# Depthwise products of images 2 to 4 from half-precision high and low parts

## The chip, the core and the metric

The kernel runs on one core of one Trainium2 chip. The metric is the device time of one execution in microseconds (us), the median of several runs. A core has five engines that run their own instruction streams and meet at semaphores: TensorE (PE, with its weight loads listed as PEld), VectorE (DVE), ScalarE (ACT), GpSimd (POOL) and SyncE (SP, which here only issues DMAs).

## The reference

Input x holds 4 images of 96 channels and 128 x 128 pixels, in 32-bit floats. Two residual layers follow one another. The change touches the first.

```
x = x + L0(groupnorm(x))      # channel attention
x = x + L1(groupnorm(x))      # five convolutions, folded into one 5x5

L0:  xn = layernorm over the channels, with weight and bias
     q  = dwconv3x3(conv1x1(xn, q_w),  q_dw)      # 96 channels
     kv = dwconv3x3(conv1x1(xn, kv_w), kv_dw)     # 48 channels: k 24, v 24
     q, k = l2norm over the 16384 pixels of each channel
     attn = softmax(q k^T * temperature)          # 8 heads, 12 x 12 each
     out  = conv1x1(attn v, proj_w)
```

dwconv3x3 is a depthwise convolution: each of the 144 channels has its own 3 x 3 kernel and is padded with zeros. It is the operation that the change rewrites.

## The kernel before

The four images go through the same stages one after another. X, the current image, stays in on-chip memory (SBUF) as 96 channels x 16384 pixels.

**Projection.** For each of 32 tiles of 4 image rows ACT normalises (L1025), PE multiplies by the folded weights (L796), ACT squares and takes roots, DVE scales by the inverse deviation (`scaled`, L1402), and POOL adds the bias and writes the tile transposed into `Q` (`biased`, L640). In `Q` the 128 partitions are the pixel columns of the image, and the free axis is 144 channels x 128 rows. DVE writes the last tile itself (L1396).

**Depthwise stage.** The convolution along the partitions is a product with a 128 x 128 matrix with three diagonals (a band matrix). One channel takes three products, one for each vertical tap, summed in PSUM: `mm` at L817, L818 and L819, all in 32-bit floats, with the moving operand shifted by one row for the upper and the lower tap. Channels go in 24 chunks of 6 (`DC`, `DK`), two chunks to a turn of the loop. Per chunk:

- DVE makes 18 band matrices by one multiplication of the taps, spread out, with a mask (`bands`, L1428); two chunks of matrices have room (`T`), so the next `bands` of a buffer waits until PE is done with the chunk two before (`s_dw`).
- PE makes 18 products into one of two pairs of PSUM banks, and waits for the matrices (`s_T`), and for the eviction and the low part of the chunk two before (`s_qd`, `s_qkl`).
- ACT stores the result (`evict`, L1065): for q and k (chunks 0 to 19) as a 16-bit high part in `HL`, for v (chunks 20 to 23) as 32-bit floats into `Q` (L1062).
- For q and k DVE stores what the rounding left as a 16-bit low part (`low_parts`, L1437). DVE's order in the loop is `bands` of chunk n, then `low_parts` of chunk n-2.

Between its evictions ACT sums the next image's rows for its statistics (L1074, L1082), which SP loads at the same time. In image 1 POOL cuts the convolution weights into parts during this stage (`split_weights`, L596 to L615); in images 2 to 4 POOL does nothing in it.

**Attention.** DVE gathers strips (L1453), PE makes q k^T from the 16-bit parts (`gram`, L845), ACT copies v into strips (`values`, L1104) that PE turns (L837), DVE and ACT make the softmax (L1482 to L1505, L1128), PE applies it (L879) and DVE adds it to X (L1514).

**Convolution.** 11 units of rows per image; PE works from 16-bit parts (L957), with DVE, ACT, POOL and DMAs making and placing the parts.

Before image 1 a setup turns the depthwise taps into the layout of the matrices (POOL L572 to L578), with a scale from `QKS` that DVE works out (L1306 to L1315). POOL starts `biased` of image 1 after its last step.

The order on each engine is written out by hand, with a semaphore for each hand-over; there is no planner.

Of the kernel before, what the change touches and what calls it, by code (L numbers as in the profile page):

```python
# [25 lines left out]
def build_program(nc, x, ln_w, ln_b, q_w, q_dw, kv_w, kv_dw, proj_w, temperature, w1, w3, w5, wd, wf, out):  # L26
    f32, f16, bf16, i32 = mybir.dt.float32, mybir.dt.float16, mybir.dt.bfloat16, mybir.dt.int32
    ALU = mybir.AluOpType
# [22 lines left out]
    BW = 129  # L51
    GR = 8
# [8 lines left out]
    WTOP = 1024.0  # L61

# [33 lines left out]
    with ctx:  # L96
# [12 lines left out]
        def plain_sem(name):  # L109
# [11 lines left out]
        Q_AT = SLOT  # L121
        WORK_AT = Q_AT + WORK
        Q = region[:, Q_AT:WORK_AT].rearrange("p (c h) -> p c h", c=CO)
# [11 lines left out]
        V = sb("V", [P, 3, 3 * CO])  # L135
        band = sb("band", [P, BW])
# [4 lines left out]
        small = sb("small", [P, 48])  # L141
# [7 lines left out]
        pq = region[:, 0:2 * AR * CO].rearrange("p (i r c) -> p i r c", i=2, r=AR)  # L149
        y1 = work[0:C, 0:AD * BANK].rearrange("p (i n) -> p i n", i=AD)  # L150
        sq = [t.rearrange("p (r c) -> p r c", r=AR) for t in (region[:, 1152:1152 + AR * C], work[:, 2048:2048 + AR * C])]
        vr, sd, rr = (work[:, a:a + AD * AR].rearrange("p (i r) -> p i r", i=AD) for a in (2432, 2448, 2464))
# [3 lines left out]

        T = work[:, 1536:1536 + 2 * DM * BW].rearrange("p (i m x) -> p i m x", i=2, m=DM)
        vT = work[:, 0:AT * P]
# [7 lines left out]
        KEPT = VPAIRS - EARLY  # L166
        vs = [t.rearrange("p (r c) -> p r c", r=VR) for t in
              [region[:, GROUPS_QK * SLOT + k * VR * VP:GROUPS_QK * SLOT + (k + 1) * VR * VP] for k in range(3)] +
# [3 lines left out]
        assert len(vs) == KEPT and GROUPS_QK * SLOT + 3 * VR * VP <= Q_AT + QK * H  # L172
        VBANK = (1, 2, 1, 2, 4, 5, 6, 7)

        Qf = region[:, Q_AT:WORK_AT]

# [61 lines left out]
        tapsum = Qf[:, 10200:10200 + QK]  # L238
# [7 lines left out]
        QKS, CLAMP, WMAX, TMAX, BMAX = 43, 44, 45, 46, 47  # L246
        MEANX, VARX, SAX, SBIX, MG2 = 23, 24, 27, 28, 29
# [35 lines left out]
        s_T = sem("band_matrices")  # L283
        s_dw = sem("depthwise_chunk")
# [49 lines left out]
        N_BOUND, N_RES, N_QKS, N_AMAX, N_WSC = 6, 9, 17, 22, 25  # L334
# [3 lines left out]
        NPOOL = 18  # L338
# [181 lines left out]
        def _(pool):  # L520
            n = [0]

            def link(ins):
# [18 lines left out]
            link(pool.memset(band[:], 1.0))  # L542
            link(pool.affine_select(out=band[:], in_=band[:], compare_op=ALU.is_ge, fill=0.0, base=1,
                                    pattern=[[-1, BW]], channel_multiplier=1))
# [20 lines left out]
            for j in range(3):  # L565
                if j == 2:
                    pool.wait_ge(s_st, N_AFF + START)
                for d in range(3):
# [5 lines left out]
                    if d:  # L574
                        turning.done(pool.tensor_tensor(V[:, j, :], V[:, j, :], turned, ALU.add))
                        pool.wait_ge(s_V, turning.value())
# [1236 lines left out]
```

## Time and profile before

| | |
|---|---|
| time of 3 runs, us | 1709.13 (1708.07 to 1710.19) |
| span of the profiled execution, us | 1706.1 (its own run time is not recorded beside it) |
| busy share of the span | PE 97%, PEld 91%, DVE 87%, ACT 60%, POOL 34% |
| mean granted TensorE clock | 0.975 of full speed |
| HBM traffic | 52.20 MB read, 25.17 MB written |

The span runs from the first to the last instruction. A busy share is the time in which at least one instruction of the engine was open; matmuls are pipelined, so a busy PE need not be at its peak. A group names the source line, the engine and the operation, then output and input, and after the bar the busy time and the mean of one instruction in ns, then the idle time before it and what ended it. The lines of the pieces are shares of the chain of work that ended last.

### The profile page before, as it was taken

How to read it: one execution, taken by the hardware profiler on the slowest of the kernel's cores; microseconds unless marked ns; L12 is line 12 of the kernel's file. 1: busy time of each engine (PE TensorE's matmuls, PEld its weight loads, DVE VectorE, ACT ScalarE, POOL GpSimd, SP SyncE). 2: the span in 40 equal slices, each digit the busy share in tenths (PEclk: the TensorE clock that was granted, in tenths of full speed). 3: DMA queues.
4: the chain of work that ended last, by engine and by line, in shares of the span. 5: the costliest groups of instructions: out<-in, count | busy, mean ns of one | idle time of the engine just before them, and what ended most of it. 6: DMA issues, size and time to landing. Idle time of an engine off the chain costs nothing.

```text
span 1706.1 us, 38231 instructions
## 1 busy us (share of the span) xinstructions
PE 1652.5 (97%) x13285; PEld 1552.1 (91%) x13285; DVE 1488.7 (87%) x1964; ACT 1022.2 (60%) x1665; POOL 579.8 (34%) x398
## 2 busy tenths in 40 slices
PE   6999999999999999999999999999999999999998
PEld 6989959999999996999999996899999999599998
DVE  6788879999888859999978886999988887799997
ACT  4856576555385658545546666755446566765551
POOL 4999931222281003232247002123326400312222
PEclk9999979999999997999999999899999999799999
DMA  7012115666502201666630220366661121055553
GB/s 192 0 47 65 38 32 136 177 164 172 153 2 61 69 19 44 157 167 172 169 95 15 69 65 1 87 165 175 167 165 46 35 73 41 1 133 139 135 144 104
DMA packets 105017, 166.01 MB, mean 97 GB/s; under 512 B 40266, under 2 KB 78763, under 8 KB 104780
## 3 DMA queue, kind: packets, MB, share of 16 engines
q1 hardware_dynamic: 81772, 138.95, 32.0%
q10 hardware_dynamic: 23168, 26.04, 4.7%
q8 instruction: 47, 0.77, 0.2%
q14 instruction: 30, 0.25, 0.0%
HBM read 52.20 MB, written 25.17 MB: 45 GB/s over the span
## 4 chain that ended last, share of the span: by engine, by line
PE 84%; DVE 7%; issue 4%; ACT 3%; DMA 1%; DVEq 0%; SPq 0%; POOL 0%; ACTq 0%; POOLq 0%
PE ps L957 41%; PE ps L796 12%; PE ps L817 8%; PE ps L819 7%; PE ps L818 7%; PE ps L845 3%; PE ps L879 3%; PE ps L952 1%; PE ps L752 1%; ACT region L1178 1%; DVE region L1706 1%; DVE region L1676 1%; ACT region L1111 1%; DVE X L1514 1%; DVE region L1673 1%
## 5 line engine op out<-in xcount | busy, mean ns | idle before, releaser
L957 PE MATMUL ps<-region,W 128*96 128x256 f16 (+2 forms) x7140 | 800.7, 270 | 10.0 <-DMA region<-region 5.4
L957 PEld LDWEIGHTS ps<-region,W 128*96 128x96 f16 (+1 forms) x7140 | 771.3, 122 | 31.8 <-issue 14.8
L1428 DVE TENSOR_TENSOR region<-V,band 128x2322 f32<-128x2322 f32 (+2 forms) x104 | 257.8, 2488 | 59.5 <-PE ps L819 56.1
L1178 ACT ACTIVATE region<-region 96x1584 f16<-96x1584 f32 (+2 forms) x80 | 98.4, 1272 | 309.1 <-DVE region L1610 309.1
L701 POOL TENSOR_TENSOR region<-region 96x528 f32<-96x528 f32 (+1 forms) x72 | 92.0, 1282 | 445.9 <-DVE region L1676 328.4
L817 PE MATMUL ps<-region 128*128 (+1 forms) x1152 | 228.1, 280 | 10.4 <-DVE region L1428 4.5
L819 PE MATMUL ps<-region 128*128 (+1 forms) x1152 | 222.8, 275 | 0.0
L818 PE MATMUL ps<-region 128*128 (+1 forms) x1152 | 222.2, 274 | 0.0
L1706 DVE SCALAR_TENSOR_TENSOR region<-ps,small,region 96x768 f32<-96x768 f32 (+1 forms) x220 | 203.7, 988 | 12.1 <-PE ps L957 10.4
L796 PE MATMUL ps<-proj,region 96*128 96x240 f32 x1024 | 209.3, 367 | 0.6 <-DVE region L1402 0.6
L796 PEld LDWEIGHTS ps<-proj,region 96*128 96x128 f32 x1024 | 194.8, 191 | 14.1 <-DVE region L1402 1.0
L640 POOL TENSOR_TENSOR region<-region,cbias 128x576 f32 (+1 forms) x124 | 175.6, 1419 | 56.7 <-DVE region L1402 53.3
L817 PEld LDWEIGHTS ps<-region 128*128 128x128 f32 x1152 | 174.6, 191 | 16.9 <-issue 15.2
L691 POOL TENSOR_TENSOR region<-region,X 96x1536 f32<-96x1536 f32 x40 | 116.1, 2903 | 197.0 <-DVE region L1737 197.0
L1676 DVE TENSOR_TENSOR region<-region 96x1056 f16<-96x1056 f32 (+6 forms) x160 | 175.4, 1154 | 0.0
L819 PEld LDWEIGHTS ps<-region 128*128 128x128 f32 x1152 | 174.8, 192 | 0.0
L818 PEld LDWEIGHTS ps<-region 128*128 128x128 f32 x1152 | 174.8, 192 | 0.0
L667 POOL TENSOR_TENSOR region<-X 96x512 f32<-96x512 f32 (+1 forms) x16 | 29.2, 1844 | 385.1 <-PE ps L879 385.1
L1065 ACT ACTIVATE region<-ps 128x768 f32 (+1 forms) x80 | 65.8, 823 | 137.2 <-PE ps L819 137.2
L1172 ACT ACTIVATE region<-region 96x1584 f16<-96x1584 f16 (+3 forms) x88 | 114.0, 1296 | 0.3
L1402 DVE TENSOR_TENSOR region<-ps,region 128x576 f32<-128x576 f32 x124 | 94.0, 758 | 15.0 <-DVE region L1392 1.9
L1025 ACT ACTIVATE region<-X,small 96x512 f32 (+1 forms) x128 | 101.6, 802 | 0.3 <-DVE small L1330 0.3
(234 smaller groups left out, 2199.8 us busy)
## 6 DMA issues: line engine op xcount, KB each, us to landing
region<-region SPq DMA_DIRECT2D x104, 247.5 KB, 3.9
region<-in_x_dram SPq DMA_DIRECT2D x128, 192.0 KB, 2.3
out_dram<-region SPq DMA_DIRECT2D x40, 576.0 KB, 4.2
region<-region ACTq DMA_DIRECT2D x72, 247.5 KB, 2.4
X<-in_x_dram SPq DMA_DIRECT2D x30, 576.0 KB, 6.2
region<-region SPq DMA_DIRECT2D x32, 247.4 KB, 4.9
X<-in_x_dram SPq DMA_DIRECT2D x19, 384.0 KB, 10.6
region<-region SPq DMA_DIRECT2D x24, 185.6 KB, 3.7
```

The source lines that it names most:

```text
L640: pool.tensor_tensor(Q[:, :, bass.ds(t * AR, AR)].rearrange("p c r -> p r c"), pq[:, i], cbias[:].unsqueeze(1).broadcast_to([P, AR, CO]), ...
L691: pool.tensor_tensor(ob[:, 0:r * W], ob[:, 0:r * W], X[:, bass.ds(u * UR * W, r * W)], ALU.add).then_inc(s_res, 1)
L796: last = mm(ps[:, 2 * i + r // 2, r % 2 * 256:r % 2 * 256 + NP], y1[:, i, r * W:(r + 1) * W], proj[:], start=True, stop=True)
L817: mm(o, T[:, i, 3 * c + 1, 0:W], src, start=True, stop=False)
L818: mm(o[:, 1:H], T[:, i, 3 * c, 0:W], src[:, 0:H - 1], start=False, stop=False)
L819: last = mm(o[:, 0:H - 1], T[:, i, 3 * c + 2, 0:W], src[:, 1:H], start=False, stop=True)
L957: last = mm(o, w, src, start=k == 0, stop=k == len(steps) - 1, skip_group_check=split and ck > 0)
L1172: act.activation(hi2[0:C, a:e, x:z], hi[0:C, a:e, x:z], ACT.Copy).then_inc(s_h, 1)
L1178: act.activation(dst[0:C, a:e, x:z], src, ACT.Copy, scale=1.0 if whole else col(SA)).then_inc(s_h, 1)
L1428: v.tensor_tensor(T[:, i, 3 * c:3 * c + m].rearrange("p m (i j) -> p m i j", j=3), taps.broadcast_to([P, m, BW // 3, 3]), mask.broadcast_t ...
L1676: v.tensor_tensor(low[:, :, x:end], src, hi[0:C, a:e, x:end], ALU.subtract).then_inc(s_l, 1)
L1706: step = lambda dst, g, factor, src: v.scalar_tensor_tensor(row(dst), product(i, g, blocks), col(factor), row(src), ALU.mult, ALU.add).the ...
```

## The change

The depthwise products of images 2 to 4 (`b` > 0) run on 16-bit operands. A value is cut into a high and a low 16-bit part, and a product of 32-bit values becomes three products: high matrix x high values, high matrix x low values, low matrix x high values. Image 1 keeps the 32-bit products.

- PE: 54 products of 16-bit operands per chunk in place of 18 of 32-bit operands.
- POOL (`query_split`): per chunk a copy of 768 values per partition into 16 bits (`QH`, two buffers), then the subtraction of it from the 32-bit values, written as 16 bits (`QL`, in the place of the chunk in `Q`). It waits until PE is done with the chunk two before. Chunk 0 goes in three parts.
- DVE (`bands`): per chunk two multiplications of 16-bit operands with 16-bit results of 18 x 132 elements per partition, in place of one with 32-bit operands of 18 x 129. The mask `band` is kept in 16 bits; taps are stored with the three horizontal taps next to each other (`V`).
- `low_parts` becomes one scalar_tensor_tensor (scale, then subtract), `evict` takes a scale; six channels lie next to each other in two PSUM banks.
- At the end of image 1's depthwise stage DVE cuts the taps into parts once (three instructions).
- Setup: DVE scales the projection weights and bias (two instructions) and keeps gains for taps and values apart; POOL's last step scales all taps (1296 elements, before 1080) and writes them in the new order.
- Buffers: `Q` begins 768 elements earlier, and between it and `work` lies room for `QH`. `pq`, `y1`, `sq` and the small statistics move. The strips of v have five buffers (before six); `values(7)` comes after the load of ACT's exponential table.

```diff
+        QH = span(EXTRA_AT, DC * H).bitcast(f16).rearrange("p (i c h) -> p i c h", i=2, c=DC)
+        QL = span(Q_AT, WORK).bitcast(f16).rearrange("p (n e) -> p n e", n=DK)[:, :, 0:DC * H].rearrange("p n (c h) -> p n c h", c=DC)
+        T16 = work[:, 1536:1536 + 2 * DM * BW16].bitcast(f16).rearrange("p (i k m x) -> p i k m x", i=2, k=2, m=DM)
...
-            turning.done(pool.tensor_scalar(V[:, :, 0:3 * QK], V[:, :, 0:3 * QK], col(QKS, P), None, ALU.mult))
+            turning.done(pool.tensor_scalar(Vf[:], Vf[:], col(TAPGAIN, P), None, ALU.mult))
...
+                def query_split(k2, i, parts):
+                    n = k2 * 2 + i
+                    done = (b - 1) * DK + n
+                    pool.wait_ge(s_dw, b * DK + n - 1 + START)
+                    for at, (c, channels) in enumerate(parts):
+                        rows = Q[:, bass.ds(n * DC + c, channels), :]
+                        high = QH[:, i, c:c + channels]
+                        step = len(PARTS_OF_T) // len(parts)
+                        pool.tensor_copy(high, rows).then_inc(s_qh, step)
+                        pool.wait_ge(s_qh, done * len(PARTS_OF_T) + (at + 1) * step + START)
+                        pool.tensor_tensor(QL[:, bass.ds(n, 1), c:c + channels].rearrange("p o c h -> p (o c) h"), rows, high,
+                                           ALU.subtract).then_inc(s_qsp, step)
+                if b > 0:
+                    pool.wait_ge(s_q, (b + 1) * (AT - 1) + START)
+                    pool.wait_ge(s_pq, (b + 1) * AT + START)
+                    query_split(0, 0, PARTS_OF_T)
+                    query_split(0, 1, ((0, DC),))
+                    with pool.Fori(1, DK // 2) as k2:
+                        for i in range(2):
+                            query_split(k2, i, ((0, DC),))
...
                                 pe.wait_ge(s_T, n * len(PARTS_OF_T) + ready + START)
+                                if b:
+                                    pe.wait_ge(s_qsp, (n - DK) * len(PARTS_OF_T) + ready + START)
...
+                            if b:
+                                high = QH[:, i, c]
+                                low = QL[:, bass.ds(k2 * 2 + i, 1), c].rearrange("p o h -> p (o h)")
+                                for tap, to, x in ((1, 0, 0), (0, 1, 0), (2, 0, 1)):
+                                    n_ = H - to - x
+                                    for part, src in ((0, high), (0, low), (1, high)):
+                                        last = mm(o[:, to:to + n_], T16[:, i, part, 3 * c + tap, 0:W], src[:, x:x + n_],
+                                                  start=(tap, part) == (1, 0) and src is high, stop=(tap, part) == (2, 1))
+                                continue
...
-                for k in range(KEPT, VPAIRS):
+                for k in range(KEPT, VPAIRS - 1):
                     values(k)
...
                 act.activation(col(TMAX), epsc[0:C, 0:1], ACT.Exp)
+                values(VPAIRS - 1)
                 act.wait_ge(s_st, sv + N_NMX + START)
...
+            link(setup, v.tensor_scalar(col(TAPGAIN, P), col(TAPGAIN, P), TAPTOP, None, ALU.mult))
+            link(setup, v.tensor_scalar(col(QGAIN, P), col(QGAIN, P), QTOP, None, ALU.mult))
+            link(setup, v.tensor_scalar(proj[:, 0:CO], proj[:, 0:CO], col(QGAIN), None, ALU.mult))
+            link(setup, v.tensor_scalar(cbias[:], cbias[:], col(QGAIN, P), None, ALU.mult))
...
+                        if b:
+                            wide = mask16.rearrange("p (i j) -> p i j", j=3).unsqueeze(1).broadcast_to([P, m, BW16 // 3, 3])
+                            for part in range(2):
+                                taps = V16[:, bass.ds(k2 * 2 + i, 1), 1 - part, 9 * c:9 * c + 3 * m] \
+                                    .rearrange("p o (m j) -> p (o m) j", j=3).unsqueeze(2)
+                                step = v.tensor_tensor(T16[:, i, part, 3 * c:3 * c + m].rearrange("p m (i j) -> p m i j", j=3),
+                                                       taps.broadcast_to([P, m, BW16 // 3, 3]), wide, ALU.mult)
+                            step.then_inc(s_T, len(PARTS_OF_T) // len(parts))
+                            continue
...
-                    v.tensor_tensor(part(GC), ps[:, 4 + 2 * i:6 + 2 * i, 0:3 * H].rearrange("p k (c h) -> p h k c", c=3), part(0),
-                                    ALU.subtract).then_inc(s_qkl, 1)
+                    v.scalar_tensor_tensor(part(GC), chunk_of(i).rearrange("p (c h) -> p h c", c=DC),
+                                           HLSCALE, part(0), ALU.mult, ALU.subtract).then_inc(s_qkl, 1)
...
+                if b < 1:
+                    whole_taps = Vf[:].rearrange("p (n e) -> p n e", n=DK)
+                    dve.wait_ge(s_T, DK * len(PARTS_OF_T) + START)
+                    v.tensor_copy(VH, whole_taps).then_inc(s_vsp, 1)
+                    dve.wait_ge(s_vsp, 1)
+                    v.tensor_tensor(V16[:, :, 0], whole_taps, VH, ALU.subtract).then_inc(s_vsp, 1)
+                    dve.wait_ge(s_vsp, 2)
+                    v.tensor_copy(V16[:, :, 1], VH).then_inc(s_vsp, 1)
```

## Rows read from the trace of the kernel before

**Rows 1.** The page: the span, and the chain that ended last by line.

```profile
span 1706.1 us, 38231 instructions
...
PE ps L957 41%; PE ps L796 12%; PE ps L817 8%; PE ps L819 7%; PE ps L818 7%; PE ps L845 3%; PE ps L879 3%; PE ps L952 1%; PE ps L752 1%; ACT region L1178 1%; DVE region L1706 1%; DVE region L1676 1%; ACT region L1111 1%; DVE X L1514 1%; DVE region L1673 1%
```

**Rows 2.** Windows, image 2's depthwise stage: length, PE, PEld, DVE, ACT, POOL, clock, DMA.

```profile
519.00:618.40 99.40, 98.42 (x866) 97.40 (x865) 80.86 (x53) 61.17 (x152) 0.04 (x1) 1.00 0.22 64
```

**Rows 3.** Timeline, both ends of that stage: start, us, engine, line.

```profile
517.65 1.34 DVE L1396 SCALAR_TENSOR_TENSOR region<-ps,region,cbias 128x144 f32<-128x144 f32 x4
...
519.19 5.20 DVE L1428 TENSOR_TENSOR region<-V,band 128x387 f32<-128x387 f32 x4 [0.20 <-DVE region L1396]
...
618.59 6.75 PE L845 MATMUL ps<-region 128*120 128x240 f16 x64
```

**Rows 4.** The chain in order of time: start, us, stretches of 16-bit products.

```profile
300.95 18.52 PE ps L957 x163
...
618.73 6.61 PE ps L845 x64
...
1688.61 6.98 PE ps L957 x83
```

**Rows 5.** Groups by shape in image 2's depthwise stage, DVE alone.

```profile
L1428 DVE TENSOR_TENSOR region<-V,band 128x2322 f32<-128x2322 f32 x23 | 59.3, 2578 | 14.8 <-PE ps L819 14.3 <-issue 0.5
...
L1437 DVE TENSOR_TENSOR region<-ps,region 128x768 f32 x20 | 19.0, 952 | 0.0
...
L1453 DVE COPY region<-region 128x1920 f16<-128x1920 f16 x4 | 2.5, 640 | 3.7 <-PE ps L819 3.7
```

**Rows 6.** Timeline of POOL in image 1's depthwise stage.

```profile
103.01 2.80 POOL L611 TENSOR_TENSOR W<-W 96x192 f32<-96x192 f32 x1
105.89 2.81 POOL L612 TENSOR_TENSOR W<-W 96x192 f32<-96x192 f32 x1
108.77 0.82 POOL L613 CAST W<-W 96x768 f16<-96x768 f32 x1
...
137.28 1.64 POOL L615 TENSOR_TENSOR W<-W 96x768 f16<-96x768 f32 x1
...
165.25 3.85 POOL L615 TENSOR_TENSOR W<-W 96x768 f16<-96x768 f32 x1
```

**Rows 7.** Timeline of the setup, POOL and DVE.

```profile
24.55 1.25 DVE L1306 TENSOR_REDUCE region<-region 128x120 f32<-128x1080 f32 x1
...
41.07 1.59 POOL L572 TENSOR_SCALAR V<-region,small 128x432 f32<-128x432 f32 x1 [5.06 <-DVE small L1330]
...
44.42 1.10 POOL L575 TENSOR_TENSOR V<-V,region 128x432 f32<-128x432 f32 x1
...
48.50 3.02 POOL L578 TENSOR_SCALAR V<-V,small 128x1080 f32<-128x1080 f32 x1
...
53.01 0.76 DVE L1402 TENSOR_TENSOR region<-ps,region 128x576 f32<-128x576 f32 x1 [1.78 <-POOL region L640]
```

**Rows 8.** Timeline of DVE in image 1's depthwise stage.

```profile
99.87 8.38 DVE L1428 TENSOR_TENSOR region<-V,band 128x387 f32<-128x387 f32 x5 [0.20 <-DVE region L1396]
108.17 0.94 DVE L1437 TENSOR_TENSOR region<-ps,region 128x768 f32 x1
...
137.84 3.52 DVE L1428 TENSOR_TENSOR region<-V,band 128x2322 f32<-128x2322 f32 x1 [1.11 <-PE ps L819]
...
164.53 3.07 DVE L1428 TENSOR_TENSOR region<-V,band 128x2322 f32<-128x2322 f32 x1 [1.33 <-PE ps L819]
```

**Rows 9.** Timeline of ACT in image 2's attention.

```profile
619.52 4.73 ACT L1104 ACTIVATE region<-region 128x384 f32<-128x384 f32 x6
...
635.75 0.20 ACT L1126 ACTIVATE small<-epsc 96x1 f32<-96x1 f32 x1
...
636.18 0.31 ACT L1128 ACTIVATE region<-region,small 96x24 f32<-96x24 f32 x1 [0.23 <-DVE small L1498]
```

**Rows 10.** Windows of image 1's depthwise stage and image 2's attention, for the clock.

```profile
640.00:656.00 16.00, 15.43 (x57) 4.44 (x50) 16.00 (x29) 13.85 (x16) 13.76 (x13) 0.65 0.01 2
...
120.00:140.00 20.00, 18.23 (x161) 17.86 (x161) 17.41 (x9) 12.79 (x34) 19.18 (x12) 1.00 0.20 59
```

More of the change, by code:

```diff
@@ L134, in build_program @@
         proj = sb("proj", [C, NP])
-        V = sb("V", [P, 3, 3 * CO])
-        band = sb("band", [P, BW])
+        Vf = sb("V", [P, 9 * CO])
+        V = Vf[:].rearrange("p (m j) -> p m j", j=3)
+        V16 = Vf[:].bitcast(f16).rearrange("p (n k e) -> p n k e", n=DK, k=2)
+        band = sb("band", [P, BW16], f16)
         ident = sb("ident", [P, P])
@@ L140, in build_program @@
         cbias = sb("cbias", [P, CO])
-        small = sb("small", [P, 48])
+        small = sb("small", [P, 52])
         nsums = sb("nsums", [C, 2 * AT])
@@ L146, in build_program @@
         ps = ctx.enter_context(nc.psum_tensor("ps", [P, 8, BANK], f32))
[L149 to L152, printed above, removed]
+        span = lambda at, n: region[:, at:at + n]
+        chunk_of = lambda i: ps[:, 4 + 2 * i:6 + 2 * i, :].rearrange("p k n -> p (k n)")[:, 0:DC * H]
+        pq = [span(at, AR * CO).rearrange("p (r c) -> p r c", r=AR) for at in (0, EXTRA_AT)]
+        SQ_AT = EXTRA_AT + AR * CO
+        Y1_AT = SQ_AT + AR * C
+        sq = [span(at, AR * C).rearrange("p (r c) -> p r c", r=AR) for at in (SQ_AT, Y1_AT + AD * BANK)]
+        y1 = region[0:C, Y1_AT:Y1_AT + AD * BANK].rearrange("p (i n) -> p i n", i=AD)
+        vr, sd, rr = (span(at, AD * AR).rearrange("p (i r) -> p i r", i=AD) for at in (576, 592, 608))
+        assert AR * CO <= 576 and 624 <= Q_AT
         stage = [work[0:C, j * BANK:(j + 1) * BANK] for j in range(3)]
@@ L165, in build_program @@
         EARLY = 2
-        KEPT = VPAIRS - EARLY
+        KEPT = 5
         vs = [t.rearrange("p (r c) -> p r c", r=VR) for t in
-              [region[:, GROUPS_QK * SLOT + k * VR * VP:GROUPS_QK * SLOT + (k + 1) * VR * VP] for k in range(3)] +
+              [span(GROUPS_QK * SLOT, VR * VP), span(EXTRA_AT, VR * VP)] +
               [work[:, AT * P + k * VR * VP:AT * P + (k + 1) * VR * VP] for k in range(3)]]
@@ L171, in build_program @@
         strip_at = lambda k: S[0] if k == 0 else S[1 + (k - 1) % 3]
-        assert len(vs) == KEPT and GROUPS_QK * SLOT + 3 * VR * VP <= Q_AT + QK * H
+        assert len(vs) == KEPT and GROUPS_QK * SLOT + VR * VP <= Q_AT + QK * H
         VBANK = (1, 2, 1, 2, 4, 5, 6, 7)
-        Qf = region[:, Q_AT:WORK_AT]
+        Qf = region[:, Q_AT:EXTRA_AT]
         RING = SLOTS * BLK
@@ L540, in _ @@
                                     pattern=[[CG, GROUPS], [0, CG]], channel_multiplier=-1))
[L542 to L546 removed]
+            link(pool.memset(wideband, 1.0))
+            link(pool.affine_select(out=wideband, in_=wideband, compare_op=ALU.is_ge, fill=0.0, base=1,
+                                    pattern=[[-1, BW16]], channel_multiplier=1))
+            link(pool.affine_select(out=wideband, in_=wideband, compare_op=ALU.is_ge, fill=0.0, base=1,
+                                    pattern=[[1, BW16]], channel_multiplier=-1))
+            link(pool.tensor_copy(band[:], wideband))
             link(pool.memset(res, 0.0))
@@ L570, in _ @@
                     turn = small[:, at:at + 1]
-                    product = turned if d else V[:, j, :]
+                    product = turned if d else V[:, :, j]
                     turning.done(pool.tensor_scalar(product, rawdw[:, :, d], turn, None, ALU.mult))
@@ L574, in _ @@
                     if d:
-                        turning.done(pool.tensor_tensor(V[:, j, :], V[:, j, :], turned, ALU.add))
+                        turning.done(pool.tensor_tensor(V[:, :, j], V[:, :, j], turned, ALU.add))
                         pool.wait_ge(s_V, turning.value())
             pool.wait_ge(s_dv, N_QKS)
-            turning.done(pool.tensor_scalar(V[:, :, 0:3 * QK], V[:, :, 0:3 * QK], col(QKS, P), None, ALU.mult))
+            turning.done(pool.tensor_scalar(Vf[:], Vf[:], col(TAPGAIN, P), None, ALU.mult))
             assert turning.n == N_TURNED
@@ L1305, in _ @@
             dve.wait_ge(s_taps, 3)
[L1306 removed]
+            link(setup, v.tensor_reduce(tapsum, rawdw.rearrange("p (c m) d -> p c (m d)", m=3), AX.X, ALU.add,
                                         apply_absolute_value=True))
@@ L1415, in _ @@
                     scaled(AT - AD + i, i, i == AD - 1)
+                mask16 = band[:]
                 def bands(k2, i, parts):
```

69 lines of the change are left out of this document (40 added, 29 removed).

## The prediction

> **What bounds the kernel now.** I read the page first: the chain that ended last runs over PE for most of its length; the largest piece is the convolution (L957), then the projection (L796), then the three lines of the depthwise products, 22% together [rows 1]. The change touches only these last. Then I cut out one depthwise stage, image 2's, by windows: PE is busy 98.42 of 99.40 us, DVE 80.86, ACT 61.17, POOL 0.04, at clock 1.00 [rows 2]. So PE is the bound there, at 98.42 / 24 = 4.10 us a chunk, and DVE is 81% full. The stage lasts from the end of L1396 (517.65 + 1.34 = 518.99) to the first gram product at 618.59: 99.6 us [rows 3]. Images 3 and 4 look the same; three such stages are changed. The question is which engine needs longest for a chunk afterwards.
>
> **PE, per chunk.** 18 products of 32-bit operands go, 54 of 16-bit operands with 128 columns come. No row has 16-bit products with 128 columns, but three dense stretches stand close: 256 columns 18.52 / 163 = 114 ns, 240 columns 6.61 / 64 = 103 ns, 192 columns 6.98 / 83 = 84 ns [rows 4]. At 2.4 columns per ns that is 107 + 7, 100 + 3 and 80 + 4. For 128 columns: 53 + 4 to 7, 57 to 60; I take 58 (nearest is the row of 192). The upper bound is 111, if the loading of 128 weight columns (another 53) were not hidden. A chunk: 54 x 0.058 = 3.13 us, bounds 3.1 and 6.0. PE alone would gain 0.97 us a chunk.
>
> **DVE, per chunk.** One band instruction goes (2578 ns for 2322 elements), two of 16 bits with 18 x 132 = 2376 elements come. The band row and the low-part row (952 ns for 768) give 1626 / 1554 = 1.046 ns an element and 149 ns fixed [rows 5]. Four band instructions of 387 + 774 + 1161 + 2322 elements would be 5.45 us by this and took 5.20 [rows 3]: each starts 0.085 before the one ahead of it ends. What a two-operand instruction costs with all operands in 16 bits, no row shows. Bounds: the 32-bit rate, 0.149 + 2376 x 1.046 ns = 2.63 us, and the rate of the 16-bit copy, 640 / 1920 = 0.333 ns an element, 0.79 us [rows 5]. The copy shows that 16-bit operands can pass several elements in the time of one of 32 bits; I take half of the 32-bit streaming time, the same bytes per ns: 0.149 + 1.24 = 1.39 us. Two of them and the low part (unchanged): 2 x (1.39 - 0.085) + 0.87 = 3.48 us, if nothing else uses the memory.
>
> The Trainium skill (VectorE: DVE Perf Modes, The perf-mode tier table) gives tensor_tensor two elements a cycle for 16-bit operands; by its figures this instruction takes about 1.4 us, and the sum would be the same.
>
> **POOL, per chunk, and the turns with DVE.** POOL is idle in the stage now; a copy into 16 bits and a subtraction with 16-bit result come. Image 1 has the same two forms with 768 elements: 0.82 us and 1.64 us, where they run free [rows 6]. These rows have 96 partitions; a 128-partition subtraction of 432 elements took 1.10 us [rows 7], which for 768 gives 1.96 as the upper bound. Free, POOL needs 0.82 + 1.64 + two gaps of 0.08 = 2.62 us a chunk, less than PE. But image 1's stage also shows what happens beside band instructions. A band instruction that starts at 137.84, while the subtraction of 137.28 still runs (until 138.92), takes 3.52 us and ends at 141.36: 2.44 after POOL is done, 0.14 less than a whole band instruction [rows 6, 8]. The other way, the subtraction of 165.25 beside the band instruction that ends at 164.53 + 3.07 = 167.60 takes 3.85 us and ends at 169.10: 1.50 after it, 0.14 less than its own 1.64. So the two do not share the memory: one waits for the whole of the other and saves only 0.14 us of its start. They take strict turns: through the run of five band instructions from 99.87 to 108.25 POOL's small instructions of 103.01 and 105.89 end 2.9 us apart, one behind each of the last two, the last 0.45 after DVE [rows 6, 8]. The low part isn't in it: L1437 at 108.17 and the copy at 108.77 overlap, and both take their usual 0.94 and 0.82 [rows 6, 8].
>
> In images 2 to 4 DVE has two band instructions and POOL two instructions a chunk, both always with the next one ready. A turn of the cycle: band 1.39 - 0.14 = 1.25, copy 0.68, band 1.25, subtraction 1.50; the low part (0.95) runs beside the subtraction. Sum 4.68 us a chunk, against 4.10 now. PE (3.13) and ACT (61.17 / 24 = 2.55) fit below it, and PE is done with a chunk before the next but one asks for its buffer, so nothing else lengthens the cycle. The gain of PE is not used: PE waits about 1.5 us in each chunk for parts.
>
> **One stage.** From 518.99: 0.2 to the first band instruction; chunk 0 in parts, like a cycle with eight more short instructions, 5.05 (estimate); 23 x 4.68 = 107.6; then PE's last chunk 3.13 and the small product after it 0.2. Sum 116.2 against 99.6: +16.6. Three stages: +49.9.
>
> **Setup, once.** DVE's reduction grows from 1080 to 1296 elements (1.25 us, +0.23) [rows 7]; three more small instructions in its chain, about 0.85 by the fixed 0.15 and 1.046 ns an element. POOL's first step of the last column waits for that chain, its last step grows from 3.02 to 3.62, and writes in the new order stand three elements apart: L572, which reads so, takes 3.7 ns an element where L575 takes 2.55 [rows 7], so up to 0.5 for each of two additions; I take 0.8. Sum 2.5, bounds 1.7 and 3. It is on the path: DVE stands 1.78 us at 53.01 for the first bias addition, which POOL starts after that step [rows 7]. DVE's cutting of the taps at the end of image 1's stage (three instructions, 2.8 us) lies beside PE's last two chunks; I count 0.5, bounds 0 and 1.
>
> **Softmax, four times.** `values(7)` (4.73 / 6 = 0.79 us) now runs after the table load, which ends at 635.95; the exponential started at 636.18 [rows 9]. It ends at about 636.75: +0.6, so 2.4 for four images. The other moves (buffers, six channels in a row, the scale in the eviction, one fewer strip buffer) change no instruction's size and add no late wait; 0.
>
> **Sum.** 49.9 + 2.5 + 0.5 + 2.4 = +55.3. The span of 1706.1 becomes 1761.4; the median of the runs lies 3.0 above the span, so 1709.1 + 55.3 = 1764 us. Own range 1745 to 1795: with 1.96 for the subtraction +22, with 0.25 us a chunk saved in the hand-overs -17.
>
> **Rivals.**
> - *No turns (faster).* The 16-bit band instructions leave POOL alone, or are so short that the turns fit. Without turns the stage is DVE's: 3.2 start, 20 x 3.48 + 3 x 3.13 (chunks without a low part, PE's pace) + 3.13 + 0.2 = 85.5, or -14.1 a stage; -42.3 + 5.4 gives 1672 us. It decides where a cycle falls below (99.6 - 1.8 - 8.6) / 23 = 3.88 us, so a band instruction below 0.99 us. For it: the copy's rate would do that. Against: all turns in rows 6 and 8 are between forms that read two operands, as these are. The Trainium skill (SBUF — State Buffer, SBUF: two separate sides) says that VectorE instructions with two SBUF inputs and GpSimd exclude one another for whole instructions, and it names no type; by it this rival falls. Chance 13%.
> - *Full-length 16-bit band instructions.* 2.63 us each: cycle 2 x 2.49 + 2.18 = 7.16, stage 0.2 + 7.5 + 164.7 + 3.3 = 175.7, +76; 1709.1 + 228 + 5.4 = 1943 us. For it: taps are spread by a repeated read of three elements, which no 16-bit row has. The Trainium skill (Vector Engine (DVE) Microarchitecture Reference, 5.1) has such instructions at one element a cycle when one element is read again and again; here three neighbours are. Chance 9%.
> - *PE becomes the bound.* Either weights aren't hidden or PE's waits of 1.5 us a chunk let its clock fall to 1.2 GHz: 111 ns a product, 6.0 us a chunk, stage 146, +46; 1709.1 + 139 + 5.4 = 1853 us. For it: clock 0.65 in a stretch with 57 products in 16 us; against it: 1.00 with PE busy 18.2 of 20 [rows 10], and here 54 dense products in every 4.7 us. Chance 7%.
> - The forecast: 71%.
>
> The range takes in the forecast's own and the faster rival, 1670 to 1800, and leaves out the other two (16%) and a little of the forecast. Within 0.2% (3.4 us, about what a measurement tells from no change) lies only a narrow piece between rival and forecast: 3%. Faster 11%, slower 86%.
>
> **What would show it.** Right: in images 2 to 4 POOL's subtractions and DVE's band instructions lengthened by each other, band instructions of about 1.4 us in their shortest, 4.7 us from chunk to chunk, PE idle about a third of the stage for POOL, stages of 116 us. Products 57 to 60 ns apart; gram of image 1 where it was, plus some 3 us. Wrong: band instructions never below 2.6 us; POOL instructions at 0.82 and 1.64 beside running band instructions; stages below 100 us; clock under 1 in the stage; or the difference outside these three stages.

## The result: 1843.9 us, slower by 7.9%

The changed kernel takes 1843.86 us (median of 4 runs, 1840.80 to 1847.21) against 1708.99 us: a ratio of 1.0787, 95% interval 1.0772 to 1.0802. The forecast was 1764 us, range 1670 to 1800. The direction was right; the loss is +135 us, not +55, and lies outside the range.

The page of the changed kernel, its first lines (busy us, share of the span, instructions; PEclk is the granted clock in 40 slices). PE falls to 6 or 7 in slices 12 to 14, 22 to 24 and 32 to 34, the depthwise stages of images 2 to 4, and there DVE stands at 9:

```profile
span 1839.1 us, 41682 instructions
...
PE 1638.7 (89%) x14581; PEld 1523.6 (83%) x14581; DVE 1666.2 (91%) x2045; ACT 1022.7 (56%) x1665; POOL 932.6 (51%) x555
...
PE   6999999999976679999997668999999777899998
...
DVE  6788889999899969999889996999988999699997
...
PEclk9999979999999997999998999799999888889999
```

Windows over the three changed stages (length, PE, PEld, DVE, ACT, POOL, clock, DMA). The first answers to [rows 2]:

```profile
525.40:667.20 141.80, 89.62 (x1299) 84.32 (x1298) 139.89 (x79) 61.35 (x152) 112.58 (x52) 0.92 0.15 45
982.00:1124.00 142.00, 91.56 (x1292) 86.10 (x1293) 138.94 (x78) 61.36 (x152) 112.80 (x50) 0.89 0.15 45
1438.00:1575.00 137.00, 96.79 (x1296) 91.97 (x1297) 132.97 (x78) 61.26 (x152) 121.90 (x51) 0.84 0.16 46
```

DVE went from 81% busy to all but full, PE from 99% to 63%: the bound has changed hands. (These busy times contain the wait for the other engine's turn.) Both ends of image 2's stage, as in [rows 3]:

```profile
523.98 1.35 DVE L1458 SCALAR_TENSOR_TENSOR region<-ps,region,cbias 128x144 f32<-128x144 f32 x4
...
667.26 0.91 PE L899 MATMUL ps<-region 128*120 128x240 f16 x7
```

From 525.33 to 667.24: 141.9 us, against 99.6. Measured the same way, images 3 and 4 take 143.4 and 138.1, against 100.0 and 100.6. That is +123.3 of the span's +133.0. Of the rest, 5.1 lies ahead of image 1's stage, 0.2 in it, and 4.4 in all that follows the four stages.

Groups of DVE in image 2's stage, busy us and mean ns, as in [rows 5]:

```profile
L1496 DVE TENSOR_TENSOR region<-V,band 128x2376 f16<-128x2376 f16 x46 | 117.1, 2588 | 0.0
L1510 DVE SCALAR_TENSOR_TENSOR region<-ps,region 128x768 f32 x20 | 18.7, 935 | 0.0
```

A mean of 2588 ns, nearly a whole 32-bit band instruction; but it mixes lengths. The timeline of image 2 shows single ones, DVE first, then POOL (start, us):

```profile
560.42 1.79 DVE L1496 TENSOR_TENSOR region<-V,band 128x2376 f16<-128x2376 f16 x1
562.14 3.21 DVE L1496 TENSOR_TENSOR region<-V,band 128x2376 f16<-128x2376 f16 x1
565.27 0.94 DVE L1510 SCALAR_TENSOR_TENSOR region<-ps,region 128x768 f32 x1
...
560.49 3.19 POOL L684 TENSOR_TENSOR region<-region 128x768 f16 x1 [0.20 <-POOL region L682]
565.68 0.82 POOL L682 CAST region<-region 128x768 f16 x1 [1.99 <-PE ps L867]
566.70 2.94 POOL L684 TENSOR_TENSOR region<-region 128x768 f16 x1 [0.20 <-POOL region L682]
```

The first band instruction has the memory to itself: 1.79 us. The subtraction asks at 560.49, waits for its end (562.21) and ends 1.47 later; the second band instruction waits for that and ends 1.67 after it. The cast then lies beside the low part and both take their usual time. A chunk is 1.71 + 1.47 + 1.67 + 0.86 = 5.71 us. Late in image 4 the order is another:

```profile
1483.81 2.36 DVE L1496 TENSOR_TENSOR region<-V,band 128x2376 f16<-128x2376 f16 x1
1486.10 2.40 DVE L1496 TENSOR_TENSOR region<-V,band 128x2376 f16<-128x2376 f16 x1
1488.42 0.94 DVE L1510 SCALAR_TENSOR_TENSOR region<-ps,region 128x768 f32 x1
...
1484.45 2.38 POOL L682 CAST region<-region 128x768 f16 x1
1487.03 2.95 POOL L684 TENSOR_TENSOR region<-region 128x768 f16 x1 [0.20 <-POOL region L682]
```

Band, cast, band, then the subtraction with the low part beside it: the forecast's order, with 5.46 us from one low part to the next in fourteen chunks in a row. (From here on "chunk" is that distance, averaged over a stage: 4.11 to 4.16 before; 5.82, 5.80 and 5.56 in images 2 to 4 after.)

PE had time to spare (start, us, in brackets the wait and whom for):

```profile
543.19 3.29 PE L867 MATMUL ps<-region 128*128 128x128 f16 x54 [1.66 <-DVE region L1510]
548.91 4.90 PE L867 MATMUL ps<-region 128*128 128x128 f16 x54 [2.43 <-DVE region L1510]
```

The first 54 products take 3.29 us, 61 ns each, at a granted clock of 1.00. The next 54 take 4.90 us, 91 ns each: PE had stood idle for 2.43 us just before them, and the granted clock of their stretch is 0.65, part of it at the lower of the two levels. Even that is below the chunk.

### The profile page after: what moved, and what is told of

Same layout as the page of the kernel before. It is cut to its first block and busy times, and to the rows that moved or that the text cites. A ratio compares the mean times of both kernels' runs of the same rounds, so it can differ in the third digit from the quotient of the medians.

```text
span 1839.1 us, 41682 instructions
## 1 busy us (share of the span) xinstructions
PE 1638.7 (89%) x14581; PEld 1523.6 (83%) x14581; DVE 1666.2 (91%) x2045; ACT 1022.7 (56%) x1665; POOL 932.6 (51%) x555
## 5 line engine op out<-in xcount | busy, mean ns | idle before, releaser
L867 PE MATMUL ps<-region 128*128 128x127 f16 (+2 forms) x3888 | 278.6, 240 | 144.5 <-DVE region L1510 89.7
L867 PEld LDWEIGHTS ps<-region 128*128 128x128 f16 x3888 | 262.6, 109 | 160.6 <-issue 122.4
L1496 DVE TENSOR_TENSOR region<-V,band 128x2376 f16<-128x2376 f16 (+3 forms) x156 | 359.8, 2353 | 3.0 <-PE ps L867 2.4
L684 POOL TENSOR_TENSOR region<-region 128x768 f16 (+2 forms) x78 | 219.8, 2818 | 14.1 <-POOL region L682 12.9
L682 POOL CAST region<-region 128x768 f16 (+2 forms) x78 | 130.4, 1672 | 45.4 <-PE ps L867 44.5
L1229 ACT ACTIVATE region<-region 96x1584 f16<-96x1584 f16 (+3 forms) x88 | 114.1, 1296 | 0.3
L1818 DVE TENSOR_TENSOR region<-region 96x256 f32<-96x256 f32 (+3 forms) x176 | 88.4, 543 | 14.8 <-DMA out_dram<-region 13.2
L1085 ACT ACTIVATE region<-ps 128x384 f32<-128x384 f32 x128 | 62.7, 490 | 54.7 <-PE ps L839 51.7
L1136 ACT ACTIVATE region<-region,small 96x512 f32<-96x512 f32 x128 | 90.8, 710 | 0.1
```

Of the source, the lines that this page charges most:

```text
L682: pool.tensor_copy(high, rows).then_inc(s_qh, step)
L684: pool.tensor_tensor(QL[:, bass.ds(n, 1), c:c + channels].rearrange("p o c h -> p (o c) h"), rows, high, ALU.subtract).then_inc(s_qsp, step)
L867: last = mm(o[:, to:to + n_], T16[:, i, part, 3 * c + tap, 0:W], src[:, x:x + n_], start=(tap, part) == (1, 0) and src is high, stop=(tap, ...
L1229: act.activation(hi2[0:C, a:e, x:z], hi[0:C, a:e, x:z], ACT.Copy).then_inc(s_h, 1)
L1496: step = v.tensor_tensor(T16[:, i, part, 3 * c:3 * c + m].rearrange("p m (i j) -> p m i j", j=3), taps.broadcast_to([P, m, BW16 // 3, 3]), ...
```

## The experiments

The first theory: the turns are as forecast, but a 16-bit band instruction takes 1.79 us by itself, since it reads the taps in runs of three. Its rivals: the whole of it is POOL's doing (alone it takes 1.39), or PE's clock sets the stage. The edits below are cut to the lines that matter, some with their values put in.

**e1_no_split**: POOL splits only the first two chunks of a stage.

```
                    query_split(0, 1, ((0, DC),))
-                    with pool.Fori(1, DK // 2) as k2:
-                        for i in range(2):
-                            query_split(k2, i, ((0, DC),))
```

> Images 2 to 4 leave out GpSimd's split from the third chunk on: the high part of the first two chunks stays in both buffers and stands in for every other chunk's high and low part, so the products are of other data; the band matrices, the products, the evictions and the low parts are those of the changed kernel. Theory A (a 16-bit band instruction of runs of three taps takes 1.79 us by itself, and the rest of its 2.4 and 3.2 us is waiting for GpSimd's turn): with GpSimd silent every full band instruction takes 1.79 us, VectorE sets the chunk at 2 x 1.79 + 0.86 = 4.44 us less the overlap of fixed parts, about 4.3, the stage is 103 to 108 us instead of 142, and the time is about 1844 - 3 x 36 = 1736 us (1725 to 1750). Rival B (alone it takes 1.39 us as forecast, GpSimd's traffic stretches all of it): chunk 3.64 us, stage 87 to 92 us, time about 1685 us. Rival C (TensorE at its reduced clock or the evictions set the chunk, not the turns): stage still over 130 us, time over 1815 us.

Measured: 1749.3 us (ratio 1.0237, 1.0220 to 1.0255); stages 110.9, 110.8, 112.0; chunk 4.28. Two neighbouring band instructions, with POOL silent:

```profile
561.31 1.80 DVE L1493 TENSOR_TENSOR region<-V,band 128x2376 f16<-128x2376 f16 x1
...
563.88 1.81 DVE L1493 TENSOR_TENSOR region<-V,band 128x2376 f16<-128x2376 f16 x1
```

Theory A holds in instruction and chunk (4.28 for "about 4.3"); the stage is 3 to 4 us over its range, since here PE waits for both first chunks' split before it starts. B and C fall. So POOL's turns cost 26 to 33 us of a stage, but even without them the changed kernel would not be faster: DVE alone needs 4.28 us a chunk where 4.11 was the pace before.

**e2_runs**: what the run length does to the instruction, POOL silent.

```
-taps = V16[:, bass.ds(k2 * 2 + i, 1), 1 - part, 9 * c:9 * c + 3 * m]
+run, stride, off = (1, 2, 0), (2, 2, 0), (4, 4, 0), (6, 6, 0), (4, 4, 1), ...
+taps = W16[:, off:off + m * stride].rearrange("p (m s) -> p m s", s=stride)[:, :, 0:run].unsqueeze(2)
```

> As e1_no_split, and the taps operand of the full 16-bit band instruction is read from the convolution weights, of other values, in runs of 1, 2, 4, 6 (image 2), 4 from an odd element, 12, 11, 33 (image 3), 132, 132 from an odd element, 3 with every map's run at an even element, and 66 (image 4); output and mask are as before, 2376 elements. Theory A (two elements a cycle, the last one of an odd run alone, so a run of r takes the whole part of (r+1)/2 cycles at 0.96 GHz): 1: 2.62 us; 2, 4, 6, 12, 66, 132: 1.39; 3: 1.80; 11: 1.50; 33: 1.42. Rival B (the run length does not matter, the offset of a map's run does: pairs need an even start): 3 at even elements 1.39, 4 and 132 from an odd element 2.6, the others 1.39. Rival C (neither matters, 1.79 is the price of three operands of 16 bits): all 1.79 but perhaps the run of 1.

Measured, single instructions (in this order: runs of 1, 2, 4, 4 from an odd element, 11, 3 from even elements):

```profile
566.89 2.63 DVE L1496 TENSOR_TENSOR region<-W,band 128x2376 f16<-128x2376 f16 x1
569.44 1.39 DVE L1496 TENSOR_TENSOR region<-W,band 128x2376 f16<-128x2376 f16 x1
563.33 1.39 DVE L1496 TENSOR_TENSOR region<-W,band 128x2376 f16<-128x2376 f16 x1
979.01 2.00 DVE L1496 TENSOR_TENSOR region<-W,band 128x2376 f16<-128x2376 f16 x1
975.39 1.50 DVE L1496 TENSOR_TENSOR region<-W,band 128x2376 f16<-128x2376 f16 x1
1388.78 1.81 DVE L1496 TENSOR_TENSOR region<-W,band 128x2376 f16<-128x2376 f16 x1
```

Runs of 6, 12 and 66 took 1.38 to 1.39, of 33 1.42, of 132 1.39, and 1.41 from an odd element. One rule, fitted to the first two of these rows, gives the others within 0.01 us: time goes with the 4-byte words that the runs of the taps touch (the other operand and the output were the same in all). From runs of 1 (2376 words) and 2 (1188): (2.63 - 1.39) / 1188 = 1.044 ns a word and 0.15 fixed. A run of three touches two words wherever it starts: 1584 words, 1.80 us. A run of 4 from an odd element touches three: 1782, 2.01. A run of 11: 1296, 1.50. Theory A gave all but the odd starts, where B is right in part: the start counts, by the words it adds. The kernel ran once, at 1727.9 us; only its single instructions are used.

**e3_long_runs**: the split as in the changed kernel, the taps in long runs; the forecast with its one wrong term put right.

```
-taps = V16[:, bass.ds(k2 * 2 + i, 1), 1 - part, 9 * c:9 * c + 3 * m]
+taps = W16[:, 0:132 * m].rearrange("p (m s) -> p m s", s=132).unsqueeze(2)
```

> The changed kernel with GpSimd's split as it is, but the taps operand of the 16-bit band instructions is read from the convolution weights, of other values, in runs of 132. Theory A (the run of three is the one term that the forecast had wrong, the turns are as forecast): band instruction 1.39 us alone, chunk 4.68 us by the forecast's order of turns and 1.31 + 1.48 + 1.26 + 0.86 = 4.91 us where the low part finds no subtraction to hide beside, stage 116 to 122 us, time 1844 - 3 x (20 to 26) = 1766 to 1784 us. Rival B (GpSimd's two passes set the chunk through the lock, whatever the band takes): stage over 135 us, time over 1820 us. Rival C (the clock and TensorE's restarts keep what VectorE gives back): stage 125 to 135 us, time 1795 to 1820 us.

Measured: 1772.4 us (1.0376, 1.0358 to 1.0393); stages 117.7, 118.6, 117.8. DVE, then POOL:

```profile
560.70 2.01 DVE L1497 TENSOR_TENSOR region<-W,band 128x2376 f16<-128x2376 f16 x1
562.64 0.94 DVE L1511 SCALAR_TENSOR_TENSOR region<-ps,region 128x768 f32 x1
563.50 1.97 DVE L1497 TENSOR_TENSOR region<-W,band 128x2376 f16<-128x2376 f16 x1
565.39 2.01 DVE L1497 TENSOR_TENSOR region<-W,band 128x2376 f16<-128x2376 f16 x1
...
561.66 2.56 POOL L684 TENSOR_TENSOR region<-region 128x768 f16 x1 [0.20 <-POOL region L682]
564.16 1.99 POOL L682 CAST region<-region 128x768 f16 x1
```

560.70 to 565.39 is 4.69 us; the forecast's turn was 4.68, in the same order, and its stage 116.2. So the run length is worth 71 us of the 135, the change of order that comes with it included, and with 1.39 us for the band instruction the forecast of the stages holds.

**e4_cast_on_act** and **e5_no_subtract**: what each of POOL's passes costs.

```
-pool.tensor_copy(high, rows).then_inc(s_qh, step)
...
+act.activation(QH[:, i, c:c + channels], Q[:, bass.ds(n * DC + c, channels), :],
+               ACT.Copy).then_inc(s_qh, len(PARTS_OF_T) // len(parts))
```

> The changed kernel, the high part (the cast to 16 bits) made by ScalarE two chunks ahead, right behind the wait of the eviction; GpSimd only subtracts. Theory A (turns: each of GpSimd's two passes takes VectorE's time): one turn of the cast, 0.66 us, goes where it was not hidden; the chunk is 2 x 1.65 + 1.50 = 4.80 us if the low part lies beside the subtraction and 5.66 us if it does not; the stage is 119 to 136 us, the time 1775 to 1835 us, the likeliest near 1790. Rival B (the cast lay beside the low part in most chunks, and ScalarE's extra 0.8 us per chunk comes into the chain of eviction and low part): stage 140 us or more, time 1840 to 1860 us.

Measured: 1818.6 us (1.0644, 1.0626 to 1.0662); stages 132.1 to 133.8, chunk 5.42 to 5.52, single ones from 4.85 to 6.30. Inside A's range and not near its likeliest: the low part lies beside the subtraction in some chunks only.

```
-pool.tensor_tensor(QL[:, bass.ds(n, 1), c:c + channels].rearrange("p o c h -> p (o c) h"), rows, high,
-                   ALU.subtract).then_inc(s_qsp, step)
...
-for part, src in ((0, high), (0, low), (1, high)):
+for at, (part, src) in enumerate(((0, high), (0, other), (1, high))):
```

> The changed kernel without GpSimd's subtraction: the low-part products read the high part of another row of the chunk, so the values are of other data; GpSimd's cast of every chunk stays. Theory A (strict turns, and a GpSimd pass that meets only the low part of VectorE, which reads PSUM, costs nothing): the cast of 0.66 us fits beside the low part of 0.86 us, the chunk is that of the kernel without a split, 4.28 us, up to 4.28 + 0.66 = 4.94 us where the cast meets a band instruction; stage 111 to 123 us, the time 1750 to 1787 us, the likeliest 1755. Rival B (each GpSimd pass costs VectorE its whole length whatever VectorE runs): 4.94 us in every chunk, stage 125 us, time about 1795 us. Rival C (the subtraction is not what costs): stage over 135 us, time over 1820 us.

Measured: 1738.0 us (1.0169, 1.0152 to 1.0186), below A's range; stages 107.1, 107.1, 108.1, chunk 4.35 to 4.40. The cast stands at its own 0.83 us beside the low part and costs next to nothing; the subtraction costs 30 to 36 us of a stage. The time was missed because I had taken e1's longer start for part of every such stage. DVE's low part, then POOL, in e5:

```profile
563.25 0.94 DVE L1507 SCALAR_TENSOR_TENSOR region<-ps,region 128x768 f32 x1
...
563.46 0.83 POOL L682 CAST region<-region 128x768 f16 x1 [3.49 <-PE ps L864]
567.82 0.83 POOL L682 CAST region<-region 128x768 f16 x1 [3.54 <-PE ps L864]
```

**e11_order**: is the step from 5.46 to 5.8 us the order of turns?

```
                        pool.wait_ge(s_qh, done * len(PARTS_OF_T) + (at + 1) * step + START)
+                        pool.wait_ge(s_T, (b * DK + n) * len(PARTS_OF_T) + (at + 1) * step + START)
```

> The changed kernel with one wait more on GpSimd: the subtraction of a chunk starts only behind the second band instruction of that chunk, so that the order of turns is the forecast's (band, cast, band, subtraction with the low part beside it). Theory A (the rest of the loss, between 5.48 us by the forecast's order with the right band instruction and the 5.7 to 5.8 us that images 2 and 3 show, is the order: there the subtraction lies between the bands and the low part has only the cast beside it): chunk 5.46 to 5.5 us in all three images, stage 134 to 137 us instead of 138 to 143, the time 1844 - 12 to 24 us = 1820 to 1832 us. Rival B (the rest is TensorE's clock and its restarts, or the subtraction now ends last before TensorE and delays it): chunk 5.7 us or more, time 1840 us or more.

Measured: 1847.8 us (1.0815, 1.0793 to 1.0837), chunk 5.82 throughout: theory A's time and chunk are missed, and the numbers are rival B's. DVE and POOL show the order as wanted, and a new price:

```profile
560.51 2.40 DVE L1497 TENSOR_TENSOR region<-V,band 128x2376 f16<-128x2376 f16 x1
...
563.10 1.64 POOL L685 TENSOR_TENSOR region<-region 128x768 f16 x1 [1.86 <-DVE region L1497]
564.68 2.38 POOL L682 CAST region<-region 128x768 f16 x1
```

The band instruction ahead ends at 562.91 (560.51 + 2.40). The subtraction starts 0.19 later, on the semaphore, and takes its whole 1.64; one that stands waiting already ends 1.47 after the band instruction. That is 0.36 a chunk, as much as the order gains. So this run does not settle whether the order alone is worth the step. That the forecast's order runs at 5.46 is seen in image 4; what flips the kernel into one order or the other is open.

**e9_all_f32**: what the change costs outside the three stages.

```
-                if b > 0:
+                if b > B:
...
-                        if b:
+                        if b > B:
```

> The changed kernel with all images' depthwise products in 32 bits (no splits of values or taps); what stays of the change is the scaling of weights and bias, the taps' order, the smaller mask in 16 bits, the fewer value buffers and the order of the softmax. Theory A (outside the changed stages 9 to 10 us are lost, of which setup 3.5 to 5.5 and the softmax 1.1 each): stages 99 to 101 us as before, the time 1715 to 1720 us; the 32-bit band instruction keeps its 2.58 us with the 16-bit mask. Rival B (the loss outside comes with the 16-bit stages, by buffers and code that they need): within 2 us of 1709. Rival C (the f16 mask's or the taps' new order lengthens the 32-bit band instruction): stages over 105 us, time over 1735 us.

Measured: 1714.5 us (1.0028, 1.0019 to 1.0037), stages 99.7, 99.6, 100.7. Just below A's 1715: 4.8 us are lost outside the stages, where A had 9 to 10. Nearly all of the loss is in the stages, and a mask in 16 bits doesn't change the 32-bit instruction:

```profile
L1498 DVE TENSOR_TENSOR region<-V,band 128x2322 f32<-128x2322 f16 x20 | 51.6, 2578 | 12.8 <-PE ps L873 12.8
```

**e6_mixed, e7_mixed_ahead, e8_mixed_values, e10_third_bank**: the runs above point to a kernel in which PE's gain fits under DVE. Only every second chunk goes in 16 bits, its taps are written twice (runs of six), and POOL is left with the one subtraction.

```
+act.activation(TAPS6[:].rearrange("p k m s j -> p (k m) s j"),
+               V16[:, bass.ds(k2, 1)].rearrange("p o k (m j) -> p (o k m) j", j=3).unsqueeze(2)
+               .broadcast_to([P, 2 * DM, 2, 3]), ACT.Copy).then_inc(s_t6, 1)
...
+if b and i == 0:
+    taps = TAPS6[:, part, 3 * c:3 * c + m].rearrange("p m s j -> p m (s j)").unsqueeze(2)
```

> In images 2 to 4 only the even chunks run in 16 bits, the odd ones in 32 bits as in the kernel before; the taps of an even chunk are written twice by ScalarE, so that the band instruction reads runs of six; ScalarE makes the high part, GpSimd only subtracts. Theory A (words and turns): a pair of chunks takes TensorE 3.29 + 4.10 = 7.4 us and VectorE 2.51 + 2 x 1.25 + 2 x 0.86 = 6.7 us, with the subtraction's turn of 1.50 us up to 8.2 us, against 8.2 us before; stage 91 to 100 us against 99.6; outside the changed stages some 9 us stay lost (setup and softmax, as in the changed kernel); the time 1690 to 1720 us, the likeliest 1705. Rival B (the turns fall so that the 32-bit band instruction, too, waits for GpSimd, and ScalarE's longer chain delays the eviction): pair 9 us or more, stage 108 us, time over 1740 us. Rival C (TensorE falls to its reduced clock in the even chunks): pair 8.2 to 9 us, time 1718 to 1745 us.

Measured: 1733.9 us (1.0147, 1.0130 to 1.0164), stages 106.7, 105.8, 107.4, a pair 8.69 us. The time falls into C's range, by another mechanism: the granted clock of the three stages is 0.97 to 1.00. PE is done with an even chunk at 557.7; then ACT's cast, POOL's subtraction and the second of the two band instructions follow one another, and the next even chunk waits 1.01 us for the low part that comes last:

```profile
557.88 0.84 ACT L1113 ACTIVATE region<-region 128x768 f16 x1 [0.59 <-PE ps L864]
...
559.02 1.72 POOL L684 TENSOR_TENSOR region<-region 128x768 f16 x1 [6.96 <-ACT region L1113]
...
563.10 3.29 PE L864 MATMUL ps<-region 128*128 128x128 f16 x54 [1.01 <-DVE region L1532]
```

```
-    high_part(k2 + 1)
...
+    high_part(k2 + 2, turn)
```

> As e6_mixed, with two buffers for the high part: ScalarE casts the next even chunk but one right behind the eviction of an odd chunk, so that GpSimd's subtraction comes a whole pair earlier, while TensorE is at another chunk. Theory A (in e6 the pair of 8.69 us was a chain: TensorE done with an even chunk, cast 0.84, subtraction's turn 1.72, second band instruction, low part 0.94, next even chunk; the engines have room): the chain without cast and subtraction is 1.31 + 1.25 + 0.86 = 3.4 us beside the odd chunk's 4.1 us on TensorE, the pair is TensorE's 7.4 to 7.7 us, stage 92 to 96 us, the time 1692 to 1706 us. Rival B (the subtraction, wherever it starts, takes its 1.5 us out of VectorE's chain): pair 8.2 us or more, stage 101 us or more, time 1718 to 1734 us.

Measured: 1719.0 us (1.0055, 1.0041 to 1.0068), stages 101.0 to 102.0, a pair 8.18 (8.29 in image 4): rival B's numbers. PE shows what is left in every pair, a wait for the low part of the 32-bit chunk before (0.87 us, 0.98 in image 4):

```profile
561.83 2.86 PE L866 MATMUL ps<-region 128*128 128x127 f16 x48
565.56 0.48 PE L871 MATMUL ps<-region 128*128 x2 [0.87 <-DVE region L1538]
```

```
+                values(VPAIRS - 1)
                act.wait_ge(s_st, sv + N_DIAG + START)
...
                act.activation(col(TMAX), epsc[0:C, 0:1], ACT.Exp)
-                values(VPAIRS - 1)
```

> As e7_mixed_ahead, and the last piece of the values is turned for the softmax before the square root, into ScalarE's wait of about 1 us for VectorE, and not ahead of the exponential. Theory A (the softmax is longer since the exponential waits behind that piece, 0.44 us, and what follows it by up to 1.4 us): 0.4 to 1.4 us less per image, the time 1.6 to 5.6 us below e7. Rival B (the piece is late there as well, since its buffer comes free only when the Gram products end): within 0.8 us of e7.

Measured: 1716.1 us (1.0036, 1.0022 to 1.0050), 2.9 below e7, as theory A has it.

```
+        bank_of = lambda b, i, turn: 0 if b and i and turn else 4 + 2 * i
...
-(k2 * 2 + i - 1 if lows else 2 * GROUPS_QK)
+(k2 * 2 + i - 1 - 2 * (b and i) if lows else 2 * GROUPS_QK)
```

> As e8_mixed_values; the 32-bit chunks put their sums by turns into the banks used so far and into a third pair of banks that is free in these stages, so that TensorE's 32-bit chunk waits for the low part of the 32-bit chunk before the last, not of the last. Theory A (the pair of 8.18 us in e7 is a loop of one 32-bit chunk on TensorE, 4.1 us, the 32-bit band matrices behind it, 2.57, and the low part, 0.95, with the hand-overs between, and the 0.87 us that TensorE waits for the low part in every pair shows it): the 0.87 us goes, the pair is 7.3 to 7.6 us, stage 92 to 95 us, the time 1716 - 3 x (6.5 to 9) = 1689 to 1697 us, below the kernel before. Rival B (the subtraction's turn, which makes the first band instruction of the even chunk wait 0.6 us, comes up as the next chain): pair 7.8 to 8.1 us, time 1700 to 1712 us.

Measured: 1700.1 us against 1709.0, ratio 0.9948 (0.9934 to 0.9963): 0.5% faster than the kernel before, and nothing is left out of it. Stages 95.7, 95.7, 95.8. Between A and B: pairs take 7.4 and 7.9 us by turns, and PE's wait for the low part, 0.87 us in every pair of e7, is 0.51 us in every second one. So 0.3 to 0.8 us of e7's 8.18 came of the loop over one pair of banks, and not of the subtraction's turn that e7's rival B had named. The window of image 2's stage shows PE at 93% and its clock full again:

```profile
524.20:619.70 95.50, 88.57 (x1083) 85.65 (x1082) 88.32 (x67) 72.74 (x178) 25.38 (x14) 1.00 0.23 67
```

## Why the prediction was right in direction and wrong in size

- *PE, 3.13 us a chunk*: 3.29. With these waits its granted clock was 0.84 to 0.92 over a stage, as the third rival had it, but PE stayed below the cycle.
- *Band instruction, 1.39 us*: **the step that failed.** It is 1.79. I took the rate of two elements a word for a stream whose source comes in runs of three; the second rival named those runs and then gave them only the whole price of 2.63. Between the two lay the right one, two words for three elements. The bounds that the prediction gave for this instruction, 0.79 to 2.63, hold 1.79; its range of the time was not worked out from them, though 0.1 us on the instruction is 2 x 0.1 x 23 x 3 = 14 us. By the Trainium skill (Vector Engine (DVE) Microarchitecture Reference, 5.1 Performance modes) a pair may span two rows of odd length where there are two sources, and 4-byte alignment makes no difference; by that the runs of three would take the 1.39 us of runs of two, as an estimate. Here they take 1.79 to 1.81, and runs of 4 take 1.39 or 2.00 by where they start; the measurement decides.
- *Strict turns, whole instructions, 0.14 saved at each hand-over*: right. Band 1.65 to 1.71, subtraction 1.47 to 1.50, cast 0.66 in their turns; e3's 4.69 for 4.68.
- *Cycle*: with 1.79 the forecast's sum is 2 x 1.65 + 0.68 + 1.50 = 5.48, and in its order the kernel runs at 5.46. That is +0.8 x 23 = 18 us a stage, 55 us in three. In images 2 and 3 the other order prevails; (5.8 - 5.48) x 23 = 7 us a stage more. Stage 116.2 forecast, 118 with the forecast's instruction (e3), 141 measured.
- *Setup, +2.5*: +5.1 in the profiled execution; the eleven experiments, with the same setup, lie between +3.4 and +5.8. Mis-sized is DVE's chain from the reduction to the last scaling. DVE, then POOL:

```profile
25.64 1.49 DVE L1363 TENSOR_REDUCE region<-region 128x144 f32<-128x1296 f32 x1
...
29.43 0.78 DVE L1375 TENSOR_SCALAR proj<-proj,small 96x144 f32<-96x144 f32 x1
30.24 0.91 DVE L1376 TENSOR_SCALAR cbias<-cbias,small 128x144 f32<-128x144 f32 x1
...
28.88 1.24 POOL L596 TENSOR_TENSOR V<-V,region 128x432 f32<-128x432 f32 x1
...
53.07 3.56 POOL L599 TENSOR_SCALAR V<-V,small 128x1296 f32<-128x1296 f32 x1
56.60 4.14 POOL L661 TENSOR_TENSOR region<-region,cbias 128x576 f32 x3
```

  The chain takes 5.5 us (25.64 to 31.15) where it took 2.9 before (24.55 [rows 7] to 27.47): +2.6, where 0.23 + 0.85 were forecast. The two scalings take 1.69. The first of them ends at 30.21, 0.09 behind POOL's addition (28.88 + 1.24 = 30.12), and in e1 it takes 1.21 and ends 0.09 behind POOL's too: here as well it seems to wait for a turn, which the forecast had only in the stage. In this execution the chain also starts 1.1 us later than before. The last step of the taps, 3.56, is as forecast.
- *Softmax, 0.6 four times*: all that follows the four stages grew by 4.4 us in sum, where 2.4 were forecast. In image 2 the exponential starts 0.44 later after the Gram products than in [rows 9], but the squares that follow start 1.4 later. e8 gives 2.9 us of it back.
- *Taps cut at the end of image 1, 0.5*: 0.2.
- *No turns; full length; PE the bound*: none came. The direction was no luck: the turns with the forecast's band instruction make the kernel slower by themselves (e3, 1772.4 us), as forecast. The real band instruction does so without turns too (e1, 1749.3 us, chunk 4.28), where the first rival, with 1.39, had 1672 us.

## What to carry to other kernels

Before a 16-bit form is counted at double rate, count the 4-byte words that a repeated operand's runs touch; a repeated run of three runs at three quarters of that rate (1188 words against 1584), and writing it twice restores it. Where VectorE multiplies two SBUF operands while GpSimd casts or subtracts there, add their lengths; each pass that GpSimd is spared, or that meets a VectorE instruction with a PSUM source, is time won. When a change makes one engine faster and loads two others, convert only as much as lets their sums meet.

## What the runs showed of the hardware

- A 16-bit product of two SBUF operands, one of them read again and again in short runs, takes 0.15 us and 1.044 ns for each 4-byte word that those runs touch: 1.39, 1.50, 1.80, 2.00 and 2.63 us for the same 2376 elements (e2).
- A GpSimd subtraction that already stands waiting ends 1.47 us behind VectorE's instruction. One that a semaphore starts behind it starts 0.19 us late and takes its whole 1.64: 0.36 us more a chunk in e11.
- A 16-bit product on 128 columns takes 61 ns at a granted clock of 1.00, and 91 in a stretch of 0.65.
- VectorE's low part, with one source in PSUM and one in SBUF, keeps its 0.94 us (0.93 to 0.96 in all runs) beside GpSimd's casts and subtractions.
